# A GAT layer and a graph-routed expert layer on one core: at most two row gathers in flight, on two semaphores that take turns

## The reference, cut to what matters

```python
h = (x @ W).reshape(N, H, C)                       # layer 1: 8 heads x 32; layer 2: 4 x 4
alpha = leaky_relu(a_src[src] + a_dst[dst], 0.2)   # 100000 edges; 131072 edges
ex = exp(alpha - amax[dst])
denom = segment_sum(ex, dst)
msg = h[src] * (ex / (denom[dst] + 1e-16))[:, :, None]
out = segment_sum(msg, dst)
```

## Time and profile before

| what | us |
|---|---|
| median of 3 executions (2727.21 to 2732.99) | 2732.33 |
| span of the profiled execution, first to last instruction | 3414.5 |
| PE busy, of that span | 2388.5 (70%) |
| DVE busy | 2070.0 (61%) |
| POOL busy | 1808.7 (53%) |
| ACT busy | 899.5 (26%) |
| packets of the gathers' queue, share of 16 DMA engines | 17.9% |

### The profile page before, as it was taken

How to read it: one execution, slowest core, us unless ns; L and a number is a source line. 1 busy time by engine, 2 the same in 40 slices (tenths; PEclk the granted TensorE clock), 3 DMA queues, 4 the chain that set the end, 5 groups by cost and what they waited for, 6 DMA issues and landing times.

```text
span 3414.5 us, 41541 instructions
## 1 busy us (share of the span) xinstructions
PE 2388.5 (70%) x11358; PEld 1456.9 (43%) x11358; DVE 2070.0 (61%) x5801; ACT 899.5 (26%) x2266; POOL 1808.7 (53%) x2002
## 2 busy tenths in 40 slices
PE   3676776888888888877747666666666766666655
PEld 2443444545554554544534333333333334333334
DVE  7577887878878888878813443434443443333457
ACT  6411111222222222214613222222222222222213
POOL 0556676656656666665552554555555545455510
PEclk9778987999988999978768887877777777777777
DMA  4334444434434444351012112112221111111147
GB/s 148 118 88 112 112 113 117 105 96 102 111 96 109 103 108 105 101 146 63 7 41 61 43 46 51 41 46 44 44 57 43 44 46 40 38 46 38 44 147 263
DMA packets 171472, 280.05 MB, mean 82 GB/s; under 512 B 46278, under 2 KB 88836, under 8 KB 171236
## 3 DMA queue, kind: packets, MB, share of 16 engines
q0 software_dynamic: 69312, 133.61, 17.9%
q1 hardware_dynamic: 101924, 143.67, 12.9%
HBM read 236.30 MB, written 40.84 MB: 81 GB/s over the span
## 4 chain that ended last, share of the span: by engine, by line
PE 34%; DVE 23%; another core or an unknown queue 20%; issue 13%; DVEq 3%; ACT 2%; POOL 2%; ACTq 1%; DMA 1%; SPq 0%
PE pb L1283 7%; PE pb L1201 7%; PE pb L1187 5%; PE pb L1172 5%; DVE x_sb L2187 2%; DVE acc L2326 2%; PE pb L1164 2%; DVE big L1520 1%; DVEq L2320 1%; PE pb L1296 1%; PE pb L1079 1%; ACTq L830 1%; DVE x_sb L1774 1%; PE pb L1270 1%
## 5 line engine op out<-in xcount | busy, mean ns | idle before, releaser
L731 POOL DMA_INDIRECT Gb<-table,idx x592 | 606.0, 1024 | 369.3 <-PE pb L1283 159.9
L1187 PE MATMUL pb<-big,early 128*128 128x512 f32 (+1 forms) x832 | 528.8, 742 | 187.8 <-ACT Gb L819 100.7
L1201 PE MATMUL pb<-early,Gb 128*128 128x256 f32 x1568 | 492.7, 464 | 117.8 <-issue 83.3
L2254 DVE TENSOR_TENSOR idx<-pb,b2B 128x256 f32<-128x256 f32 x196 | 83.1, 424 | 774.1 <-remote 475.9
L1283 PE MATMUL pb<-Gb,Sall 128*128 128x264 f32 x1184 | 414.0, 453 | 49.4 <-DVE big L1520 27.2
L665 POOL DMA_INDIRECT dl<-table,idx x288 | 276.1, 959 | 314.6 <-DVE tmr L2309 134.2
L1201 PEld LDWEIGHTS pb<-early,Gb 128*128 128x128 f32 x1568 | 345.8, 233 | 222.7 <-issue 130.4
L2187 DVE TENSOR_SCALAR x_sb<-iota,x_sb 128x576 bf16<-128x576 f16 x1024 | 402.0, 432 | 0.3 <-PE pb L1173 0.3
L665 POOL DMA_INDIRECT tab<-table,idx x272 | 267.1, 982 | 237.6 <-DVE iota L2309 82.0
L731 POOL DMA_INDIRECT early<-table,idx x288 | 290.2, 1008 | 171.7 <-PE pb L1283 78.2
L1172 PE MATMUL pb<-x_sb 128*128 128x512 bf16 x1024 | 368.5, 401 | 6.9 <-DVE x_sb L2187 3.7
(11 more groups left out here) (427 smaller groups left out, 3670.5 us busy)
## 6 DMA issues: line engine op xcount, KB each, us to landing
Sall<-dlT SPq DMA_DIRECT2D x214, 256.0 KB
Y<-idx SPq DMA_DIRECT2D x96, 256.0 KB
big<-Y SPq DMA_DIRECT2D x16, 1024.0 KB, 11.0
x_sb<-in_x_dram SPq DMA_DIRECT2D x8, 1536.0 KB
Gb<-table,idx POOLq DMA_INDIRECT x592
early<-table,idx POOLq DMA_INDIRECT x560
out_dram<-x_sb SPq DMA_DIRECT2D x24, 256.0 KB
dl<-table,idx POOLq DMA_INDIRECT x288
```

The lines of the kernel that those rows point to most:

```text
L731: g.indirect_dma_start(out=G1[i % 3][:, k, :], out_offset=None, in_=g1.table, in_offset=bass.IndirectOffsetOnAxis(ap=g1.idx[:, c:c + 1], a ...
L1187: t = pe.matmul(pbank[b][:, 0:nt * 128], W1s[:, w, k, f * 128:f * 128 + 128], xT[:, t0:t0 + nt, k * 128:k * 128 + 128], start=k == 0, stop ...
L1201: t = pe.matmul(pbank[b][:, 0:D], hh[:, bi % 2, f, j * 128:j * 128 + 128], W2s[:, w, f, :], start=f == 0, stop=f == 3)
```

## The change

A gather may start only when the gather two before it has landed. For that the semaphores no longer belong to buffers: the gathers of a graph count through, even ones add 16 to the first semaphore, odd ones to the second, and gather `c` waits until semaphore `c % 2` has reached `16 * (c // 2)`. The readers on DVE wait on both semaphores for all gathers up to the end of their group, with two waits in place of one. Nothing else changes: the buffers, their releases, the order of instructions and all other engines stay as they are.

```diff
+FLIGHT = 2
...
-        l_g = sems("l_g0 l_g1 l_g2")
+        l_g = sems(" ".join(f"l_g{k}" for k in range(FLIGHT)))
...
-        main2["l_g"], tail2["l_g"] = sems("l_gg0 l_gg1 l_gg2"), sems("l_gz0 l_gz1 l_gz2")
+        main2["l_g"], tail2["l_g"] = (sems(" ".join(f"{n}{k}" for k in range(FLIGHT))) for n in ("l_gg", "l_gz"))
...
                 for k in range(W2):
                     c = i * W2 + k
+                    o = c - base * W2
+                    if o >= FLIGHT:
+                        g.wait_ge(m["l_g"][o % FLIGHT], 16 * (o // FLIGHT))
                     g.indirect_dma_start(out=Gt2[s][:, k, :], out_offset=None, in_=g2.table,
-                                         in_offset=bass.IndirectOffsetOnAxis(ap=g2.idx[:, c:c + 1], axis=0)).then_inc(m["l_g"][s], 16)
+                                         in_offset=bass.IndirectOffsetOnAxis(ap=g2.idx[:, c:c + 1], axis=0)).then_inc(m["l_g"][o % FLIGHT], 16)
...
                     if i >= 3 and k % 4 == 0:
                         g.wait_ge(p_sum, ((i - 3) * CG + k + 4) // 2)
+                    if c >= FLIGHT:
+                        g.wait_ge(l_g[c % FLIGHT], 16 * (c // FLIGHT))
                     g.indirect_dma_start(out=G1[i % 3][:, k, :], out_offset=None, in_=g1.table,
-                                         in_offset=bass.IndirectOffsetOnAxis(ap=g1.idx[:, c:c + 1], axis=0)).then_inc(l_g[i % 3], 16)
+                                         in_offset=bass.IndirectOffsetOnAxis(ap=g1.idx[:, c:c + 1], axis=0)).then_inc(l_g[c % FLIGHT], 16)
...
-                v.wait_ge(l_g[e % 3], 16 * CG * (e // 3 + 1))
+                for k in range(FLIGHT):
+                    v.wait_ge(l_g[k], 16 * (((e + 1) * CG - k + FLIGHT - 1) // FLIGHT))
...
-                v.wait_ge(m["l_g"][i % 3], 16 * W2 * (len([k for k in range(base, i + 1) if k % 3 == i % 3])))
+                for k in range(FLIGHT):
+                    v.wait_ge(m["l_g"][k], 16 * (((r + 1) * W2 - k + FLIGHT - 1) // FLIGHT))
```

## The result

The changed kernel takes 3391.43 us (3377.24 to 3400.58, 4 runs) against 2729.77 of before on the same chip: a ratio of 1.242, 95% interval 1.239 to 1.245, or 662 us more. Slower was forecast, but 259 us of it, and the time lies outside the range of 2820 to 3190.

What follows compares the result with a forecast made beforehand. POOL's gather stream was taken to be at its limit in both gather stages, hidden by its 53% busy share. 2732 plus 184 for graph 1 and 75 for graph 2 gave 2991 us, range 2820 to 3190.

Steps and rivals of the forecast that it cites:

- What bounds the kernel: Both gather stages: POOL's stream at its limit, unknown-queue stretches only the profile's cost; 1224 and 1090 us without them.
- L + w: Each pair of gathers: landing time behind the start plus POOL's time to resume, against 2.5 to 2.64 us today.
- L with quiet DMA engines: Undisturbed gathers, read from their packets: landing 2.42 us behind the start in graph 1, 2.07 in graph 2.
- w: POOL's time to resume after a landing: 0.26 us, taken from a DVE step; bounds zero and 0.56.
- The sum, term by term: Graph 1: 880 gathers at 1.60 make 1408 us, +184; graph 2: 1052 plus 112 of holds make 1164, +75.
- Waits on the readers: DVE's extra wait for 162 groups, at most 42 us, and 212 half groups on POOL with two waits: taken as nothing.
- L beside other transfers: Gathers beside broadcasts land 1.22 us later, 3 of 8 in graph 1; about 130 holds, 112 us, in graph 2.
- (a): Rival: landings stay near quiet 2.42 us in graph 1 and are hidden in both graphs; 2732 us as before; chance 0.08.
- (b): Rival: resuming on POOL also pays the 0.30 us pause, so each pair takes 0.30 more; 3183 us; chance 0.12.
- (c): Rival: fewer gathers in the DMA rings land sooner and unknown-queue stretches shrink; faster, about 2690 us; chance 0.04.
- the idle time ended by landings and DVE's waits: Signs: gathers, not issue or PE, end POOL's idle time before graph 1's gathers; DVE's L1540 reader waits often.
- A pitch in quiet stretches over 1.40: Sign of being wrong about POOL's time to resume: gathers in quiet stretches follow each other at over 1.40 us.

Runs made afterwards that it cites:

- the second profile of the kernel before: The unchanged kernel run once more for a profile to set beside the first one: 2728.13 us, profiled span 2726.4 us.

## Why the prediction was wrong in size

**What bounds the kernel** held. The three choices there were that POOL's stream is at its limit though it is busy for half the time, that the stretches of an unknown queue are no part of the timed executions, and that graph 1 and graph 2 then last 1224 and 1090 us; the second profile of the kernel before shows 1233 and 1118 and a stream in which 821 of 880 gathers follow at once. The reason given for the second was wrong, though: it isn't a cost of profiling. (The 268 us of pauses are 270 by its own rows, which changes nothing.)

**The mechanism** held: landings set the pace, and graph 1 and graph 2 add. The rule itself, (L + w) over the number in flight against POOL's own 1.32, ranks the runs with one to four in flight, but it is too low wherever L varies: with three in flight and the L of 3.31 us that graph 1 has there in the mean it gives 1.19, under 1.32, and that run took 1.47 for a gather.

**The step that failed is "L with quiet DMA engines".** It took the last packet for the landing. The landing that releases POOL is the semaphore's, whose events the trace keeps beside the packets and the waiters, and the run with one in flight shows it 2.8 us behind the start in graph 1 and 2.4 in graph 2, where the prediction had 2.42 and 2.07: 0.38 and 0.33 more. The quiet pair is then 2.8 + 0.26 = 3.06 in graph 1 and 2.66 in graph 2, over today's 2.50 in both, while the prediction found it hidden in graph 2. Half of the difference falls on each gather, 167 and 137 us for the two graphs. The range failed with it: its upper end came from w (rival b), and the quiet reading of L had no bounds at all.

**w** was right at 0.26, where the gather itself carries the wait.

**The sum, term by term.** The changed kernel's trace has the semaphores' events, from which L follows for nearly every gather: 3.18 us in the mean of graph 1, where the prediction had 2.95, and 2.75 in graph 2, where its 1.40 for a gather stand for 2.54. With them the stream can be replayed on paper: a gather starts 0.30 us behind the end of POOL's work on the one before, or 0.26 behind the landing of the one two before, whichever is later, each with its own measured L. This is a calculation from one trace, not a run (us from the first start to the last):

| | graph 1 | graph 2 |
|---|---|---|
| predicted | 1408 | 1164 |
| (L + w) / 2 with the measured mean of L | 1513 | 1252 |
| replay, each gather with its own L | 1556 | 1309 |
| the same, 0.74 in place of 0.26 where the landing's wait stands in an instruction of its own | 1613 | 1325 |
| measured | 1625 | 1341 |

The first step, 193 us, is L in the mean. The second, 100 us, has no term in the prediction, which let the buffers even out jitter: with two in flight a late landing holds back everything behind it, and an early one brings little forward, so a mean L isn't enough. The third, 73 us, is the next paragraph. The last, 28 us, stays open. The same replay gives 1272 and 1119 us for three in flight, against 1291 and 1137 measured.

**"Waits on the readers"** took nothing for the halves of groups that wait for two things (they are 214, not 212), and graph 2 has 49 such gathers too, the first of a group. There the start comes 0.48 us later than where the gather carries the landing's wait. The replay puts 57 us on those of graph 1, and turning the order round there gave back 57 us.

**"L beside other transfers"** was too large in what it was for. It put 3/8 x 1.22 = 0.46 us on each L of graph 1 for the broadcasts, 201 us of the stage; leaving them out took 0.12 off the mean L and gave back 53 us. In graph 2 leaving out half of the transfers gave back 77 us; 112 had been put on all of them. By luck this error hid a part of the first: the mean L is short by 0.23 and 0.21 us only, where the quiet one is by 0.38 and 0.33. What makes single landings late beside broadcasts (the run with one in flight reaches from 2.7 to 7.5 us) no run separated.

**The rivals.** (a) is out: landings aren't hidden, and the rule of the Trainium skill's page "DMA: Bandwidth & Descriptors", section "Anatomy of one DMA", comes out low here. It gives 2.31 and 2.04 us for the two sizes; the semaphores show 2.8 and 2.4. The same section of the Trainium skill says that most of the fixed time is the confirmation of the last byte, ahead of which the semaphore can't fire. The trace has the semaphore behind the last packet too, but by 0.34 us of the 2.8 only, which isn't most of it; whether a packet's own record holds a part of that confirmation the trace doesn't say. (b) came nearest in size, 3183, for a wrong reason: not the pause of 0.30 is added, but the 0.34 from packet to semaphore. That it lies nearer than the forecast is luck. (c) didn't occur where the kernel before takes 2730 us; for the other chip see below.

Of the signs named beforehand, the idle time ended by landings and DVE's waits are as described for graph 1. In graph 2 it isn't a few gathers that are held but 587 of 832. "A pitch in quiet stretches over 1.40" came true as the sign of being wrong: it is 1.5. The profiled span grew less than the timed executions only on paper, from 3414.5 to 3393.1 us, since the first profile was a disturbed one; against the second, of 2726.4, it grew by 667.

## What to carry to other kernels

A limit on transfers in flight is a pitch: the time from start to the semaphore, plus what the waiting engine needs to start, over the number in flight. Compare it with the issuing engine's own pitch, on quiet and on late transfers; here that is 2.8 + 0.26 us at best. Over 2, against 1.32, it came to a quarter of the kernel's time, over 4 to 0.35%. Where landings vary even the mean is too kind: three in flight, at (3.31 + 0.26) / 3 = 1.19, still cost 5%. Read the landing from the semaphore or from somebody who waited for it and not from the last packet, and where an instruction has two waits, let it carry the one that comes last.

## What the runs showed of the hardware

- From the last packet of a gather to the start of the gather that waits for it pass 0.60 us, and 1.10 if that wait stands in an instruction of its own. 0.34 of both lie ahead of the semaphore's last event (one in flight, graph 1); behind a DVE step a gather starts in 0.26.
- A gather lands later the more are in flight: 3.02, 3.18 and 3.31 us behind its start in the mean of graph 1 with one, two and three, and 2.62, 2.75 and 2.80 in graph 2.
- A wait that is already met costs next to nothing: with four in flight some 1700 waits on POOL and three more for each group on DVE, with 89 landings still late, came to 9 us.
- One chip of the three used in the experiments ran the kernel before in 3398.75 us. Its profile with three in flight has the stretches of the first profile again, in which DVE and ACT wait for up to 23 us while POOL goes on and the trace names nobody that holds them (chain by line, window 142:3290, two rows of the timeline, and one of the list of waits):

```profile
by line: another core or an unknown queue 18.9%; issue 13.6%; PE pb L1289 9.3%; PE pb L1207 8.8%; PE pb L1193 7.2%; PE pb L1178 6.2%; PE pb L1170 2.1%; PE pb L1302 1.8%; POOL Gb L737 1.7%; DMA Gb<-table,idx 1.5%; DVE acc L2334 1.4%; DMA ear
...
1776.00 0.42 DVE L2261 TENSOR_TENSOR idx<-pb,b2B 128x256 f32<-128x256 f32 x1 [14.99 <-remote]
...
1782.32 0.69 ACT L825 ACTIVATE Gb<-pb,b1c 128x512 f32<-128x512 f32 x1 [18.24 <-remote]
...
ACT Gb L825 <- remote: 576.9, 64, 21.4
```

The first profile's span of 3414.5 us lies near that chip's 3398.75, so it may be from such a chip; the record doesn't name the one it was taken on.

On that chip two in flight with the waits turned round took 3341.94 us, a ratio of 0.982 (0.977 to 0.988) to before, and 10 us more than the 3331.63 of the same kernel elsewhere. Its profile has the stretches hardly any more (chain by engine, and the same row of the waits):

```profile
DMA 57%; issue 14%; POOL 13%; DVE 6%; PE 6%; another core or an unknown queue 1%; ACT 1%; ACTq 1%; DVEq 1%; POOLq 0%; SPq 0%
...
ACT Gb L825 <- remote: 44.2, 5, 13.4
```

So on this chip they did shrink under the limit, from 18% of the chain with three in flight to 1% with two, which is the effect that rival (c) named, and the kernel gained 57 us over before. There is one profile of each, and no run tells whether it is fewer gathers in flight that does it or only the slower pace of PE that comes with them; what the stretches are stays open too. No version tried beats the kernel before where that takes 2730 us.
